# Local-attention conv block on one core: scores over 96 near keys in column tiles, P placed by ScalarE, conv filters summed in PSUM

## What is computed

```
perceived = depthwise 3x3 conv(x, w_perc) + b_perc            # 128 -> 384 channels
hid       = gelu(perceived @ w_up1.T + b_up1)                 # 384 -> 256
h         = x + hid @ w_up2.T + b_up2                         # 256 -> 128
q, k, v   = h @ w_qkv.T + b_qkv
scores    = [q . k(neighbour dy,dx)] / sqrt(128), 9 neighbours, zero padded borders
out       = h + sum(softmax(scores)[i] * v(neighbour i))
```

## Time and profile before

| | before |
|---|---|
| median of 3 runs | 483.28 us (482.9 to 489.4) |
| the profiled execution | 483.21 us, its span 481.4 us |
| TensorE matmul busy | 92% of the span |
| TensorE weight load busy | 81% |
| VectorE busy | 76% |
| ScalarE busy | 48% |
| GpSimd busy | 41% |
| mean granted TensorE clock | 0.98 of full speed |
| HBM traffic | 29.0 MB, mean 60 GB/s |

### The profile page before, as it was taken

How to read it: one execution, slowest core, us unless ns; L and a number is a source line. 1 busy time by engine, 2 the same in 40 slices (tenths; PEclk the granted TensorE clock), 3 DMA queues, 4 the chain that set the end, 5 groups by cost and what they waited for, 6 DMA issues and landing times.

```text
span 481.4 us, 8443 instructions
## 1 busy us (share of the span) xinstructions
PE 443.8 (92%) x2964; PEld 388.9 (81%) x2964; DVE 367.3 (76%) x728; ACT 230.4 (48%) x491; POOL 197.2 (41%) x154
## 2 busy tenths in 40 slices
PE   1448899999999999999999999999999999999994
PEld 1437789797979899797979899797979899797863
DVE  5998768878695968878695968778695968765644
ACT  2443264554627454553627454553627354552633
POOL 3555636354451525354451525354452525320201
PEclk9966999999999999999999999999999999999999
DMA  8101020403103040403103040403013020301011
GB/s 283 70 0 60 0 103 0 146 2 100 47 21 126 2 146 0 145 0 105 40 17 128 0 145 0 145 0 113 32 26 119 0 87 0 89 9 38 0 46 44
DMA packets 11509, 29.31 MB, mean 61 GB/s; under 512 B 2400, under 2 KB 3168, under 8 KB 11488
## 3 DMA queue, kind: packets, MB, share of 16 engines
q1 hardware_dynamic: 10784, 29.03, 17.8%
q10 hardware_dynamic: 704, 0.02, 0.1%
HBM read 20.65 MB, written 8.39 MB: 60 GB/s over the span
## 4 chain that ended last, share of the span: by engine, by line
PE 81%; issue 4%; ACT 2%; DVE 1%; POOLq 0%; POOL 0%; ACTq 0%; DVEq 0%
PE m_ps L359 38%; PE work L372 11%; PE work L431 9%; PE s_ps L401 8%; PE work L378 5%; PE work L383 5%; PE work L417 3%; PE s_ps L397 2%; ACT hid L545 0%; ACT thi L529 0%; ACT p_sb L590 0%; DVE y L738 0%; POOLq L84 0%; POOL p_sb L919 0%; ACT L590 0%
## 5 line engine op out<-in xcount | busy, mean ns | idle before, releaser
L359 PE MATMUL m_ps<-thi,whi 128*128 128x256 f32 x576 | 188.6, 327 | 15.0 <-POOL wlo L928 7.1
L359 PE MATMUL m_ps<-tlo,whi 128*128 128x256 f32 x576 | 164.1, 285 | 0.0
L359 PE MATMUL m_ps<-thi,wlo 128*128 128x256 f32 x576 | 164.1, 285 | 0.0
L359 PEld LDWEIGHTS m_ps<-thi,whi 128*128 128x128 f32 x576 | 111.2, 193 | 23.3 <-issue 14.9
L919 POOL TENSOR_TENSOR p_sb<-p_sb,rsum 128x768 f32<-128x768 f32 x31 | 45.5, 1468 | 176.3 <-DVE rsum L780 176.3
L359 PEld LDWEIGHTS m_ps<-tlo,whi 128*128 128x128 f32 x576 | 111.6, 194 | 7.2 <-issue 7.2
L359 PEld LDWEIGHTS m_ps<-thi,wlo 128*128 128x128 f32 x576 | 111.2, 193 | 0.0
L912 POOL TENSOR_TENSOR tlo<-t,thi 128x1088 fp32r<-128x1088 f32 (+1 forms) x32 | 64.2, 2027 | 44.4 <-ACT thi L529 44.4
L590 ACT ACTIVATE p_sb<-s_ps,negmax 128x197 f32<-128x197 f32 x124 | 51.4, 423 | 37.6 <-DVE negmax L773 37.6
L607 ACT ACTIVATE q_sb<-work,bq_s 128x512 f32<-128x512 f32 x32 | 22.0, 689 | 85.2 <-PE work L378 85.1
L372 PE MATMUL work<-hid,w2T 128*128 128x512 f32 x120 | 54.1, 593 | 1.5 <-ACT hid L545 1.5
(11 more groups left out here) (110 smaller groups left out, 663.9 us busy)
## 6 DMA issues: line engine op xcount, KB each, us to landing
xp<-x_planes SPq DMA_DIRECT2D x16, 680.0 KB, 5.2
xr<-x_rows SPq DMA_DIRECT2D x16, 512.0 KB, 4.0
out<-o_sb SPq DMA_DIRECT2D x32, 256.0 KB, 4.1
w1T<-w SPq DMA_DIRECT2D x1, 384.0 KB, 3.3
mask_bf<-masks SPq DMA_DIRECT2D x1, 192.0 KB, 3.9
w2T<-w SPq DMA_DIRECT2D x1, 128.0 KB, 4.9
wqk_in<-w_qk SPq DMA_DIRECT2D x1, 128.0 KB, 4.8
ident<-identity SPq DMA_DIRECT2D x1, 64.0 KB, 4.8
```

What stands on the lines that cost most here:

```text
L359: last = pe.matmul(m_ps[:, b, col:col + S], a[:, j, dy, half * P:(half + 1) * P], c[:, par, T_PLACE[j], dy * WIN:dy * WIN + S], start=(s = ...
```

## The change

It has two parts.

**Attention.** A query row only needs the 96 pixels of its three rows. The score tile of 128 queries is now made by four matmuls of 32 queries (one row) by 96 pixels; each writes its own 32 partitions of the bank (L404), so that each uses 32 columns of the TensorE array. Four tiles share a bank (STEP is 128), so `scores`, `row_max` and the mask matmul work on groups of 4 tiles. P has 101 columns a tile instead of 197. The transposes on TensorE (`transpose_p`), ScalarE's `take_pt` and VectorE's `edges` are gone. VectorE turns all of P in blocks of 32x32 (`turn_p`, into `ptc`), and ScalarE places the 12 blocks of (query row, key row) with 12 copies of 32 partitions (`place_p`) into `pt`. `values` waits for all 12 copies of both groups.

**Start.** The filter values are no longer transformed on 9-element vectors. Instead the three taps are each multiplied with `w1T` and summed (9 products a tap, three banks of PSUM in `m_ps`, `work`, `s_ps`, the first product by ScalarE, the others by VectorE), and the six sets come from the three sums by additions of 768 columns. ScalarE's first wait is for `w1T` alone; the fp32 identity is no longer loaded.

Its core (new functions in full):

```diff
-KEYS = WINDOW + NZ
-STEP = 256
+NEAR = 3 * W
+KEYS = NEAR + NZ
+STEP = P
# TensorE
-            def scores(n, j):
...
-                for u in range(2):
-                    i = 2 * j + u
-                    last = pe.matmul(s[:, u, 0:WINDOW], q_sb[:, i * P:(i + 1) * P],
-                                     h_around[:, i * P:i * P + WINDOW], start=False, stop=(u == 1),
-                                     skip_group_check=True)
+            def scores(n, g):
+                if from_image(n, 2):
+
+                    pe.wait_ge(p_done, n * 8 + (4 * g - 12))
+                s = s_bank(g)[:, :, 0:NEAR]
+                pe.matmul(s, ident_bf[:, :], mask_bf[:, g:g + 4, :], start=True, stop=False, skip_group_check=True)
+                for u in range(4):
+                    for row in range(TR):
+                        q = ((4 * g + u) * TR + row) * W
+                        last = pe.matmul(s[row * W:(row + 1) * W, u, :], q_sb[:, q:q + W], h_around[:, q:q + NEAR],
+                                         start=False, stop=(u == 3 and row == TR - 1), skip_group_check=True)
                 last.then_inc(s_ready, 1)
-            def transpose_p(n, g):
...
-                pe.wait_ge(pt_done, n * 2 + (g - 3))
-                pe.wait_ge(edges_done, n * 4 + (2 * g - 6))
+                pe.wait_ge(z_done, n * 4 - 4)
+                pe.wait_ge(pt_done, n * PLACED - PLACED)
# TensorE's body
                 units(0)
-                if store:
-                    transpose_p(n - 1, 1)
-                units(1)
+                units(1, 2, 3)
                 if store:
                     values(n, 0)
-                units(2)
-                if store:
                     values(n, 1)
-                units(3)
...
-                    scores(n, 2)
-                units(8)
-                if attn:
-                    scores(n, 3)
-                units(9, 10, 11)
-                if attn:
-                    transpose_p(n, 0)
+                units(8, 9, 10, 11)
# ScalarE
-            def take_pt(n, g):
...
+            def place_p(n):
+
+                if isinstance(n, int) and n == 1:
+                    act.wait_ge(zeroed, 3)
+                act.wait_ge(ptc_done, n * 2)
+                if from_image(n, 2):
+                    act.wait_ge(o_ready, n * 2 - 2)
+                for row in range(TR):
+                    for dk in range(3):
+                        shift, near = divmod(row + dk - 1, TR)
+                        first, end = max(0, -shift), min(T, T - shift)
+                        col = (near + 2 - dk) * W
+                        nc.scalar.copy(pt[near * W:(near + 1) * W, first + shift:end + shift, col:col + W],
+                                       ptc[row * W:(row + 1) * W, first:end, dk * W:(dk + 1) * W]).then_inc(pt_done, 1)
# VectorE
-            def edges(n, g):
+            def turn_p(n, g):
...
+                tiles = slice(4 * g, 4 * g + 4)
+                nc.vector.transpose(ptc[:, tiles, :], p_sb[:, tiles, 0:NEAR]).then_inc(ptc_done, 1)
# VectorE's body
-                if attn:
-                    sums(n, 1)
-                    edges(n, 0)
                 if conv:
                     combine(n, 1)
+                if attn:
+                    turn_p(n, 0)
+                    sums(n, 1)
+                if conv:
                     combine_y(n, 1)
+                if attn:
+                    turn_p(n, 1)
                 if conv:
                     finish_y(n, 1)
-                if attn:
-                    edges(n, 1)
# VectorE's start
+            for k, i in enumerate(TAPS):
+
+                dve.wait_ge(first_done, 3 * (k + 1))
                 for m in (1, 2):
                     for dy in range(3):
...
+                        to = tap0 if i == 0 and m == 2 else acc[i]
+                        nc.vector.scalar_tensor_tensor(out=to[:, dy, :], in0=w1T[:, m, :],
+                                                       scalar=wg[:, m, dy, i:i + 1], in1=acc[i][:, dy, :],
+                                                       op0=ALU.mult, op1=ALU.add).then_inc(acc_done, 1)
```

More of the change, by code:

```diff
@@ L580, in take_pt @@
-            def take_pt(n, g):
-                act.wait_ge(pt_ready, n * 2 + (g - 1))
-                nc.scalar.copy(pt[:, 4 * g:4 * g + 4, W:W + P],
-                               work[:, 1 + g, :].rearrange("p (t q) -> p t q", t=4)).then_inc(pt_done, 1)
+            act.wait_ge(filters_done, 1)
+            for i in TAPS:
+                first_products(i)
+            act.wait_ge(acc_done, 6)
+            nc.scalar.mul(whi[:, 0, :, :], tap0, -1.5).then_inc(whi_done, 1)
+            high_t(0, 0)
@@ new lines, in _ @@
+            act.wait_ge(sums_done, 2)
+            nc.scalar.mul(whi[:, 5, :, :], acc[2], -6.0).then_inc(whi_done, 1)
+            for i, j in enumerate((1, 3, 2, 4)):
+                act.wait_ge(weff_done, i + 1)
+                nc.scalar.copy(whi[:, j, :, :], weff[j]).then_inc(whi_done, 1)
+            act.wait_ge(wt_ready, 1)
+            act.wait_ge(b1_ready, 1)
+            wa = work[:, 2, :]
+            nc.scalar.copy(wvT[:, 0:C], wv_in[:, :]).then_inc(wt_copied, 1)
+            nc.scalar.mul(wqk[:, :], wa[:, C:2 * C], SCALE).then_inc(wt_copied, 1)
@@ L693, in _, with low_weights, low_end @@
-            for i, j in enumerate(M_ORDER):
+            def low_weights(j, k):
+                dve.wait_ge(whi_done, k)
+                nc.vector.tensor_tensor(wlo[:, j, :, :], weff[j], whi[:, j, :, :].bitcast(F32),
+                                        ALU.subtract).then_inc(wlo_dve_done, 1)
+            def low_end(j, tap, by, k):
+                dve.wait_ge(whi_done, k)
+                nc.vector.scalar_tensor_tensor(out=wlo[:, j, :, :], in0=tap, scalar=by,
+                                               in1=whi[:, j, :, :].bitcast(F32), op0=ALU.mult,
+                                               op1=ALU.subtract).then_inc(wlo_dve_done, 1)
@@ L704, in _ @@
+                if k == 0:
                     transform_ab(0, 0)
+                if k == 1:
+                    transform(0, 0)
                     dve.wait_ge(weights_in, 16 * N_W)
                     nc.vector.tensor_copy(bq_wide[:, :], bqk[:, 0:1].to_broadcast([P, P])).then_inc(bq_wide_done, 1)
[L707 to L710 removed]
+                    dve.wait_ge(acc_done, 12)
+                    nc.vector.tensor_tensor(sum02, tap0, acc[2], ALU.add).then_inc(sums_done, 1)
+                    nc.vector.scalar_tensor_tensor(out=mix02, in0=tap0, scalar=0.25, in1=acc[2], op0=ALU.mult,
+                                                   op1=ALU.add).then_inc(sums_done, 1)
@@ new lines, in _ @@
+            dve.wait_ge(acc_done, 18)
+            dve.wait_ge(sums_done, 2)
+            nc.vector.tensor_tensor(weff[1], sum02, acc[1], ALU.add).then_inc(weff_done, 1)
+            nc.vector.scalar_tensor_tensor(out=weff[3], in0=acc[1], scalar=-0.5, in1=mix02, op0=ALU.mult,
+                                           op1=ALU.subtract).then_inc(weff_done, 1)
+            nc.vector.tensor_tensor(weff[2], sum02, acc[1], ALU.subtract).then_inc(weff_done, 1)
+            low_weights(3, 4)
+            nc.vector.scalar_tensor_tensor(out=weff[4], in0=acc[1], scalar=0.5, in1=mix02, op0=ALU.mult,
+                                           op1=ALU.subtract).then_inc(weff_done, 1)
@@ L831, in body @@
                     transform_ab(n + 1, 1 - par)
+                if from_image(n, 2) and conv:
+                    combine(n, 0)
                 if store:
@@ L840, in body @@
                     add_h(n, 1)
-                if from_image(n, 2):
-                    if conv:
-                        combine(n, 0)
-                    if attn:
-                        sum_h(n, par)
+                if from_image(n, 2) and attn:
+                    sum_h(n, par)
                 if conv:
```

250 lines of the change are left out of this document (85 added, 165 removed).

## The result

After the change the kernel takes 557.73 us (median of 4 runs, 557.24 to 559.53) beside 483.61 for the kernel before on the same chip (482.9 to 489.4). The ratio is 1.151, 95% interval 1.142 to 1.160: slower, by 74 us. The forecast was 548, range 495 to 582.

The account below looks back on a forecast made before the run. The loop from one `values` to the next was to bind, with TensorE waiting: 42 + 15 x (26.6 + S + c) + 22.3 + S = 546.6 us of span, plus 1.8 around it, forecast 548, range 495 to 582.

Parts of the forecast that it names:

- 26.6 + S + c: Period of one image, `values` to next `values`: 26.6 us of loop plus small score matmuls plus clock loss.
- S: TensorE's time for an image's 32 small score matmuls (64 records), inside the loop: taken as 3.8 us.
- c: Loss per image from TensorE's clock falling after the hole ahead of `values`: 1.5 us, bounds 0 and 2.2.
- Where the time goes: TensorE ahead of `values` waits 3.7 us with nothing to do, in every image, for ScalarE's copies.
- its own sign: Stated sign of being wrong: a group of 32 small score records on TensorE takes about 0.7 us.
- Rival B: Small score matmuls overlap four ways, S = 1.3, little clock loss: 486 us (508 with c = 1.5); chance 0.11.
- The forecast's own premise: The loop binds, small score tiles overlap partly or not: 507 to 580 us; chance 0.62.
- The copies: ScalarE's 12 copies into `pt`: 0.30 us each, 3.65 in all, bounds 2.3 and 4.8.
- `combine_y`: VectorE's four operations of 256 columns in the loop, slowed beside GpSimd: 3.6 us, bounds 1.4 and 4.3.
- Rival C: Loop closes in time and TensorE binds: 456 us at S = 2.6, 475 at 3.8, 496 at 5.1; chance 0.17.
- The start: Filter setup before the first `up`: first `up` at 42 us, gain 14 us, bounds 5 and 17.
- The end: From the last `up`, where no conv units hide the loop: 22.3 + S us.

Follow-up runs that it names:

- The run at full clock: Changed kernel with two more conv units ahead of `values`, VectorE's second transpose ahead of `combine_y`, next transform and `add_h` ahead of `combine`: 470.93 us.
- 4: Changed kernel with 1 of the 12 copies of `place_p` kept and 11 left out, attention output incomplete: 465.36 us.
- 3: Changed kernel with VectorE's transpose of group 1 moved ahead of `combine_y` of half 1: 508.47 us.
- experiment 2: Changed kernel with the small score matmuls' two loops swapped, four in a row on the same 32 array columns: 584.43 us.
- 7: Changed kernel with the 12 copies replaced by 6 of 128 partitions by 256 contiguous columns, attention output not computed: 487.78 us.
- 8: Changed kernel with the 12 copies replaced by 6 of 128 partitions by 8 pieces of 32 columns, attention output not computed: 489.41 us.
- 5: Changed kernel with GpSimd's differences of the next image waiting for VectorE's `combine_y` of half 1: 523.58 us.
- 10: Changed kernel with conv units and VectorE's transpose, transform and `add_h` reordered, GpSimd's differences waiting for `combine_y`: 458.69 us, ratio 0.946 to the kernel before.
- the warm run: Changed kernel with 22 unused mask matmuls added ahead of `values` in 14 images: 536.18 us.
- 1: Kernel before with the new start alone, its attention untouched: 473.33 us, ratio 0.973.

## Why the forecast was right

The mechanism was the forecast one, and the period closes by its own terms. For the image shown, forecast 26.6 + S + c: with the measured S of 1.8 (2 x 1.06 from mask to mask, less the masks' 0.32), `values` 2.05 longer at half clock than the 2.85 of the prediction, and copies of 5.04 + 0.05 instead of 3.65, it is 26.6 + 1.8 + 2.05 + 1.44 = 31.9, and 31.9 is measured. (The 2.85 is a small slip: by its own rows it is 5.31 - 2.12 - 0.26 = 2.93. The run at full clock gives 2.84.)

- **Where the time goes:** TensorE waits for ScalarE's last copy in all 16 images: 4.8 to 5.0 us in the first 13, where 3.7 was forecast, and 3.2, 7.4 and 9.5 in the last three, where the steady loop has ended. Right, with the size off by the copies. One copy instead of twelve (4) and the early transpose (3) show that the loop is what binds.
- **S:** forecast 3.8 with bounds from 1.3; measured 1.8. This step was wrong. I let the order of the two records of a matmul limit the overlap to 2.6 at best and then took the middle to 5.1; the rows of experiment 2 show full overlap, 17 records started in the time of 5, four every 0.083 us, which makes 64 x 0.083 / 4 = 1.3. The other 0.5 is going from the mask to the small matmuls (0.25 instead of 0.16) and back (the next mask starts 0.2 behind the last four). By its own sign (a group of about 0.7 us would show it wrong) the measured 0.80 is nearly there, against 1.9 a group as forecast. The Trainium skill's factor of 4 (TensorEngine Tiling (Array Packing), Theoretical Speedup) was the better guide, and these rows agree with it: four records start where one would. Rival B's premise thus came true, and its time, 486 to 508, did not: it was right on S and had the copies and the clock too low. The forecast's own premise, that the tiles overlap partly or not, was false, although its time was met. S oversized by 2.0 is -32 us over 16 images.
- **The copies:** forecast 0.30 each, measured 0.42 (7 and 8 show 0.31 for 128 partitions, the shape of the copies in the earlier trace rows). 1.4 an image, +21 us. The upper bound of 4.8 was passed: a price taken from rows of another number of partitions.
- **`combine_y`:** forecast 3.6, measured 3.71; GpSimd as the reason is shown by 5 and 10. Rival C needed this at 1.4 together with copies at 0.19: 5 alone took 34 us off, and the kernel still took 524.
- **The clock:** forecast 1.5 an image. The mean over the images is 32.3 - 26.6 - 1.8 - 1.44 = 2.5, and `values` alone shows it: 2.05 and 2.86 above 2.85 by turns. That is above the upper bound of 2.2, and gross +15 us; the warm run gives back 1.5 an image, since another wait stands behind it.
- **The start:** forecast 42, measured 42.8: 13.3 us earlier than before, where 14 was forecast, and alone (1) a gain of 12.7 us.
- **The end:** forecast 26.1, measured 555.6 - 527.2 = 28.4: -2.0 for S, +1.4 for the copies, +2.15 for `values` at half speed, and 0.8 that I have not traced.
- **The sum:** 0.8 + 15 x (32.3 - 31.9) + 2.3 = 9 us above the forecast span of 546.6. That it is so close owes much to luck: -32 for S and +21 and +15 for copies and clock cancel.

Open: whether the 32 partitions or the change of partitions makes the copies slow; and in version 2, 0.3 of the period of 25.65 us. Its other 0.55 above TensorE's 24.8 is a wait for the copies, so the loop still binds there: they start at 239.23 behind the second transpose (238.62), which itself waits 0.94 us for GpSimd's scaling of P.

## What to carry to other kernels

When work moves from the engine that binds to others, lay out the new chain from one consumer to its next use and compare it with the bound engine's own time; here the chain was 31.9 us against 24.8, and the cure was not less work but the order: conv units over the copies, the transpose ahead of work nobody waits for, and a third engine held back while a link of the chain runs. A price for an instruction should come from rows of the same form, the number of partitions included. And a hole in TensorE's stream is to be charged twice, for itself and for the work behind it, unless that work is covered by the next wait.
